# A DCN ranking kernel: row fetches for ScalarE, copies of transposed values for VectorE, another order on TensorE

## What is computed

```python
D = 26 * 64
x0 = emb[ids].reshape(ids.shape[0], -1)          # ids past the table take its last row
x = x0
for i in range(3):
    s = x @ cross_w[i]
    x = x0 * s[:, None] + cross_b[i] + x
h = relu(x0 @ w1 + b1)      # 1664 -> 1024
h = relu(h @ w2 + b2)       # 1024 -> 512
h = relu(h @ w3 + b3)       # 512 -> 256
y = sigmoid(concatenate([x, h], axis=1) @ out_w + out_b)
```

## Time and profile before

| | us |
|---|---|
| median of 3 runs | 549.64 (549.58 to 550.9) |
| the profiled execution | 547.23 |
| its span, first to last instruction | 545.4 |
| TensorE busy (matmul) | 478.0 (88%) |
| GpSimd busy | 391.6 (72%) |
| VectorE busy | 182.8 (34%) |
| ScalarE busy | 103.8 (19%) |

### The profile page before, as it was taken

How to read it: one execution, slowest core, us unless ns; L and a number is a source line. 1 busy time by engine, 2 the same in 40 slices (tenths; PEclk the granted TensorE clock), 3 DMA queues, 4 the chain that set the end, 5 groups by cost and what they waited for, 6 DMA issues and landing times.

```text
span 545.4 us, 10919 instructions
## 1 busy us (share of the span) xinstructions
PE 478.0 (88%) x2876; PEld 438.4 (80%) x2876; DVE 182.8 (34%) x380; ACT 103.8 (19%) x187; POOL 391.6 (72%) x412
## 2 busy tenths in 40 slices
PE   0079599999989989997999989999899989999997
PEld 0069499998978879896888979788798968888896
DVE  5464623232242323223332312323232233323324
ACT  6486511011011111101111101111111011111111
POOL 5777567777777777777777777777777777777730
PEclk9999899999999999999999989999999999999999
DMA  7992111111111111111111111111111111111100
GB/s 231 223 360 74 22 25 28 26 29 28 27 28 26 30 26 29 29 28 29 27 27 30 28 29 29 26 28 28 26 28 29 30 25 29 28 26 28 27 14 2
DMA packets 20608, 25.15 MB, mean 46 GB/s; under 512 B 10135, under 2 KB 11122, under 8 KB 20546
## 3 DMA queue, kind: packets, MB, share of 16 engines
q0 software_dynamic: 12960, 13.30, 13.6%
q1 hardware_dynamic: 6288, 10.94, 5.9%
q10 hardware_dynamic: 1298, 0.21, 0.2%
HBM read 24.41 MB, written 0.01 MB: 45 GB/s over the span
## 4 chain that ended last, share of the span: by engine, by line
PE 57%; POOL 14%; DMA 11%; DVE 9%; issue 8%; ACT 2%; POOLq 0%; DVEq 0%; ACTq 0%
PE l_bank L700 45%; POOL x_raw L334 14%; DMA x_raw<-in_L_rec_emb,idx 10%; PE h_bank L700 5%; PE x_bank L714 4%; DVE x_raw L510 4%; DVE h L529 3%; PE l_bank L774 1%; ACT w_hi L352 1%; PE h_bank L785 1%; ACT h_bank L362 1%; DVE w_lo L495 1%; DMA ids<-in_r_ids 0%; PE h_bank L740 0%; DVE h1T_lo L522 0%
## 5 line engine op out<-in xcount | busy, mean ns | idle before, releaser
L334 POOL DMA_INDIRECT x_raw<-in_L_rec_emb,idx x405 | 390.7, 965 | 131.1 <-issue 108.8
L700 PE MATMUL l_bank<-w_hi,xT_hi 128*128 128x342 f32 (+1 forms) x624 | 144.8, 333 | 8.2 <-DVE xT_lo L517 8.2
L700 PE MATMUL l_bank<-w_lo,xT_hi 128*128 128x342 f32 (+1 forms) x624 | 139.0, 323 | 0.0
L700 PE MATMUL l_bank<-w_hi,xT_lo 128*128 128x342 f32 (+1 forms) x624 | 138.7, 323 | 0.0
L700 PEld LDWEIGHTS l_bank<-w_hi,xT_hi 128*128 128x128 f32 x624 | 105.4, 193 | 10.9 <-issue 5.0
L700 PEld LDWEIGHTS l_bank<-w_lo,xT_hi 128*128 128x128 f32 x624 | 108.1, 193 | 0.0
L700 PEld LDWEIGHTS l_bank<-w_hi,xT_lo 128*128 128x128 f32 x624 | 107.2, 191 | 0.0
L510 DVE COPY_PREDICATED x_raw<-past,end_row 128x256 f32<-128x256 int32 (+3 forms) x65 | 40.5, 624 | 164.2 <-DMA x_raw<-in_L_rec_emb,idx 164.0
L398 ACT ACTIVATE xT_hi<-x_bank 128x512 fp32r<-128x512 f32 (+3 forms) x66 | 33.5, 507 | 270.5 <-PE x_bank L714 263.3
L714 PE MATMUL x_bank<-identity,x_raw 128*128 128x128 f32 x208 | 35.0, 280 | 46.3 <-DVE x_raw L510 28.8
L714 PEld LDWEIGHTS x_bank<-identity,x_raw 128*128 128x128 f32 x208 | 23.9, 142 | 58.2 <-issue 57.6
(11 more groups left out here) (83 smaller groups left out, 280.8 us busy)
## 6 DMA issues: line engine op xcount, KB each, us to landing
ids<-in_L_rec_emb SPq DMA_DIRECT2D x896, 0.2 KB
w_raw<-in_L_rec_w SPq DMA_DIRECT2D x18, 512.0 KB, 22.2
ids<-in_L_rec_emb ACTq DMA_DIRECT2D x512, 0.2 KB
x_raw<-in_L_rec_emb,idx POOLq DMA_INDIRECT x405, 2.5
b_rows<-in_L_rec_b SPq DMA_DIRECT2D x1, 512.0 KB, 7.5
b_rows<-in_L_rec_b SPq DMA_DIRECT2D x1, 256.0 KB, 5.7
ids<-in_r_ids SPq DMA_DIRECT2D x1, 208.0 KB, 2.6
b_rows<-in_L_rec_b SPq DMA_DIRECT2D x1, 128.0 KB, 6.7
```

Source lines behind the costliest of these rows:

```text
L334: pool.indirect_dma_start(out=dst, out_offset=None, in_=emb, in_offset=rows).then_inc(landed, 16)
L700: done = pe.matmul(bank[:, 0:b - a], x[:, k, :], w[:, k, a:b], start=(k == 0 and n == 0), stop=(k == last_k and n == 2))
```

## The change

- GpSimd gathers 399 fields instead of 405. SyncE fetches field 24 of nine tiles, with 32 registers a load and byte addresses. ScalarE fetches field 25 of eight tiles, 32 registers a load, one field after the other.
- From tile 1 on ScalarE does nothing but these fetches up to the last tile. Its copies of transposed values (x, h1, h2) and of the side buffers become VectorE copies, each right before the VectorE subtraction that needs it. In the last tile the copies of transposed values are ScalarE's again.
- The end row is copied into the last 64 columns of the PSUM bank `x_bank[1]`, and `make_whole` reads it there.
- Groups are of 4, 3, 4 and 2 chunks. In the last tile chunk 12 comes before chunks 9 to 11.
- TensorE's list: the first half of l2 of the tile before stands ahead of the transposition of group 0, which waits for `h3_ready`; a transposition of rows stands one or two chunks before the end of the group before; layer 3 comes at the end of the next tile and writes into `x_bank[0]`.
- GpSimd's wait for `l3_done` moves from field 6 to field 16.
- The end: layer 2's first half of columns is finished first, its transposition lies in the second half, the second half is transposed in two single chunks, and the last sum of the last tile is done by ScalarE with its sigmoid.

The diff, cut to its core:

```diff
-    SIZES = [4, 4, 3, 2]
+    SIZES = [4, 3, 4, 2]
...
-    LAST_SIZES = [4, 3, 2, 2, 1, 1]
-    LAST_GROUPS = [list(range(sum(LAST_SIZES[:g]), sum(LAST_SIZES[:g + 1]))) for g in range(len(LAST_SIZES))]
-    assert sum(LAST_SIZES) == K1
+
+    LAST_GROUPS = [[0, 1, 2, 3], [4, 5, 6], [7, 8], [12], [9, 10], [11]]
+    assert sorted(sum(LAST_GROUPS, [])) == list(range(K1))
...
-    SP_TILES = [3, 5, 7, 9, 11, 13, 15]
+    SP_TILES = [2, 4, 6, 8, 9, 10, 12, 14, 15]
+    SP_REGS = 32
...
-    ACT_TILES = [4, 7, 10, 13]
+    assert SP_FIELD // FPK in GROUPS[-1] and SP_FIELD // FPK in LAST_GROUPS[3]
+    ACT_RUNS = [[3, 5], [6, 8, 10], [11, 13], [14]]
+    ACT_TILES = sum(ACT_RUNS, [])
     ACT_FIELD = F - 1
     ACT_BUFS = 2
-    ACT_REGS = 16
-    ACT_SHARES = [12, 4, 8, 8, 12]
-    assert ACT_FIELD // FPK in GROUPS[-1] and all(
-        sum(ACT_SHARES) * (t - 1) >= P * (j + 1) for j, t in enumerate(ACT_TILES)) and ACT_TILES[-1] < TILES - 1
+    ACT_REGS = 32
+    assert ACT_FIELD // FPK in GROUPS[-1] and TILES - 1 not in ACT_TILES
...
+        end_bank = x_bank[1][:, 512 - E:512]
...
-        l3_bank = h_bank[1]
+        l3_bank = [x_bank[0]] * (TILES - 1) + [h_bank[1]]
...
-                for p in range(0, P, len(regs)):
-                    sync.load(regs, sp_idx[i:i + 1, p:p + len(regs)])
+                for p in range(0, P, SP_REGS):
+                    regs = [sync.alloc_register(f"sp_row{i}_{p + j}") for j in range(SP_REGS)]
+                    sync.load(regs, at_bytes[at_row[t]:at_row[t] + 1, p:p + SP_REGS])
                     for j, reg in enumerate(regs):
-                        row = sync.snap(reg, min_val=0, max_val=H - 1)
-                        sync.dma_start(sp_rows[i % SP_BUFS][p + j:p + j + 1, :],
-                                       emb[bass.DynSlice(row, 1), :]).then_inc(sp_landed[i % SP_BUFS], 16)
-            sync.wait_ge(result_ready, 1)
+                        at = sync.snap(reg, donate=True, min_val=0, max_val=(H - 1) * ROW)
+                        sync.dma_start(sp_rows[i % SP_BUFS][p + j:p + j + 1, :].bitcast(U8),
+                                       emb_bytes[:, bass.DynSlice(at, ROW)]).then_inc(sp_landed[i % SP_BUFS], 16)
...
-                if f == 6 and t > 2:
-                    pool.wait_ge(l3_done, t - 1)
                 if f == 14:
                     pool.wait_ge(l1_done, len(PIECES) * (t - 1) + 1)
                 if f == 16:
                     pool.wait_ge(h1_transposed, 2 * t)
+                    pool.wait_ge(l3_done, t - 1)
                     pool.wait_ge(x_transposed, NG * t + 1)
...
+            def fetch(j):
+
+                if j >= ACT_BUFS:
+                    act.wait_ge(act_placed, j - ACT_BUFS + 1)
+                row = len(SP_TILES) + j
+                for p in range(0, P, ACT_REGS):
+                    regs = [act.alloc_register(f"act_row{j}_{p + i}") for i in range(ACT_REGS)]
+                    act.load(regs, at_bytes[row:row + 1, p:p + ACT_REGS])
+                    for i, reg in enumerate(regs):
+                        at = act.snap(reg, donate=True, min_val=0, max_val=(H - 1) * ROW)
+                        act.dma_start(act_rows[j % ACT_BUFS][p + i:p + i + 1, :].bitcast(U8),
+                                      emb_bytes[:, bass.DynSlice(at, ROW)]).then_inc(act_landed[j % ACT_BUFS], 16)
...
-            act.wait_ge(sp_idx_ready, 2)
-            for t in range(1, TILES - 1):
-                step(t)
+            act.wait_ge(sp_idx_ready, 1)
+            for j in range(len(ACT_TILES)):
+                fetch(j)
             last_step(TILES - 1)
             act.wait_ge(logits_ready, 1)
-            act.activation(result[:, :], logits[:, :], ACT.Sigmoid).then_inc(result_ready, 1)
+            act.activation(result[:, 0:TILES - 1], logits[:, 0:TILES - 1], ACT.Sigmoid).then_inc(result_ready, 1)
+            act.wait_ge(h3_read, TILES)
+            act.activation(result[:, TILES - 1:TILES], h3_dots[:, TILES - 1:TILES], ACT.Sigmoid,
+                           bias=term[:, TILES - 1:TILES]).then_inc(result_ready, 1)
...
-                                    end_row[:, :].rearrange("p (o e) -> p o e", o=1).broadcast_to([P, n, E])).then_inc(x_whole, 1)
+                                    end_bank.rearrange("p (o e) -> p o e", o=1).broadcast_to([P, n, E])).then_inc(x_whole, 1)
+
+            def x_hi(t, g):
+                dve.wait_ge(x_transposed, NG * t + g + 1)
+                ks = groups(t)[g]
+                dve.tensor_copy(xT_hi[:, ks[0]:ks[-1] + 1, :].rearrange("p k b -> p (k b)"),
+                                x_bank[g % 2][:, 0:len(ks) * P]).then_inc(xT_hi_ready, 1)
+
+            def relu_hi(bank, cols, hi, done):
+                dve.tensor_scalar(hi, bank[:, 0:cols], 0.0, None, ALU.max).then_inc(done, 1)
+
+            def h1_hi(t):
+                for half in range(2):
+                    dve.wait_ge(h1_transposed, 2 * t + half + 1)
+                    relu_hi(h_bank[half], HB * P, h1T_hi[:, half * HB:(half + 1) * HB, :].rearrange("p k b -> p (k b)"), h1T_hi_ready)
+
+            def h2_hi(t):
+                dve.wait_ge(h2_transposed, t + 1)
+                relu_hi(h_bank[0], K3 * P, h2T_hi[:, :, :].rearrange("p k b -> p (k b)"), h2T_hi_ready)
+
+            def place(rows, t, field, placed):
+                dve.tensor_copy(x_buf[t % 2][:, field * E:(field + 1) * E], rows).then_inc(placed, 1)
+
+            def sp_place(t):
+                i = SP_TILES.index(t)
+                dve.wait_ge(sp_landed[i % SP_BUFS], 16 * P * (i // SP_BUFS + 1))
+                place(sp_rows[i % SP_BUFS], t, SP_FIELD, sp_placed)
+
+            def act_place(t):
+                j = ACT_TILES.index(t)
+                dve.wait_ge(act_landed[j % ACT_BUFS], 16 * P * (j // ACT_BUFS + 1))
+                place(act_rows[j % ACT_BUFS], t, ACT_FIELD, act_placed)
...
+            def step(t):
+                make_whole(t, 0)
+                x_hi(t, 0)
                 x_lo(t, 0)
+                l2_out(t - 1)
                 make_whole(t, 1)
-                l2_out(t - 1)
+                x_hi(t, 1)
                 x_lo(t, 1)
+                h2_hi(t - 1)
+                h2_lo(t - 1)
                 make_whole(t, 2)
-                h2_lo(t - 1)
+                x_hi(t, 2)
                 x_lo(t, 2)
-
-            def step(t):
-                begin(t)
+                if t in SP_TILES:
+                    sp_place(t)
+                if t in ACT_TILES:
+                    act_place(t)
                 make_whole(t, 3)
-                l3_out(t - 1)
+                x_hi(t, 3)
                 x_lo(t, 3)
                 l1_out(t)
                 dots_out(t)
-                make_whole(t + 1, 0)
+                h1_hi(t)
                 h1_lo(t)
+                l3_out(t - 1)
...
+                if g == 0 and t > 1:
+                    pe.wait_ge(h3_ready, t - 1)
...
+            def l2_last(t, half, ks):
+                for k in ks:
+                    if half == 0 and k % QB == 0:
+                        pe.wait_ge(h1T_ready, 2 * t + 1 + k // QB)
+                    for n, (x, w) in enumerate(((h1T_hi, w2_hi), (h1T_hi, w2_lo), (h1T_lo, w2_hi))):
+                        done = pe.matmul(L2_LAST[half][:, 0:NH], x[:, k, :], w[:, k, half * NH:(half + 1) * NH],
+                                         start=(k == 0 and n == 0), stop=(k == K2 - 1 and n == 2))
+                    if k == K2 - 1:
+                        done.then_inc(l2_done, 1)
...
+            def ahead(t):
+                return 1 if t >= TILES - 2 else 2
...
-
+                l2(t - 1, range(0, HB))
                 transpose_x(t, 0)
-                l2(t - 1, range(0, HB))
+                l2(t - 1, range(HB, K2))
                 l1(t, 0, slice(0, 1))
-                l2(t - 1, range(HB, K2))
+                transpose_h2(t - 1)
+                l1(t, 0, slice(1, -ahead(t)))
                 transpose_x(t, 1)
-                l1(t, 0, slice(1, 3))
-                transpose_h2(t - 1)
-                l1(t, 0, LAST)
-                l1(t, 1, slice(0, 1))
-                transpose_x(t, 2)
-                l3(t - 1)
-                l1(t, 1, slice(1, None))
+                l1(t, 0, slice(-ahead(t), None))
 
             def step(t):
                 begin(t)
+                for g in range(1, NG):
+                    l1(t, g, slice(0, -ahead(t)))
+                    if g < NG - 1:
+                        transpose_x(t, g + 1)
+                    l1(t, g, slice(-ahead(t), None))
+                transpose_h1(t)
+                l3(t - 1)
+
+            def last_step(t):
+                begin(t)
+                l3(t - 1)
+                l1(t, 1, BODY)
+
+                pe.wait_ge(h3_ready, t)
+                transpose_x(t, 2)
+                l1(t, 1, LAST)
                 transpose_x(t, 3)
                 l1(t, 2)
+                transpose_x(t, 4)
                 l1(t, 3)
-                transpose_h1(t)
-
-            def last_step(t):
```

(22 more changed lines are left out.)

186 lines of the change are left out of this document (75 added, 111 removed).

## The result

The changed kernel takes 574.07 us (571.45 to 579.51) against 550.27 us for the kernel before: the ratio is 1.044, 95% interval 1.037 to 1.052. I had forecast 542.5. It is slower, by 24 us, and 32 us above my forecast.

The account below looks back on a forecast made before the run. GpSimd's gathers were taken as the bound from tile 3 on. Gathers and TensorE's remaining work gave a 534.1 us span, the late field 4.1 more (538.2), and run and median corrections 542.5 us; range of 8 in 10: 536 to 552.

Parts of the forecast that it names:

- the sum: Gathers to tile 14, then TensorE's remaining work: span 534.1 us, 538.2 with the late field, 542.5 at the median.
- 3.4 us later: Tile 14: TensorE transposes group 2 at 479.8 us, 3.4 us after the gather of field 21 starts at 476.4.
- from tile 3 on its gates open 1 to 6 us early: GpSimd's waits on TensorE cost nothing from tile 3 on; it loses 2.1 us once, in tile 2.
- the late field: Tile 14's field fetched by ScalarE lands by 489.6 us, needed by 485.5: 4 us late, added to the end in full.
- ScalarE can't keep the pace: Rival, ScalarE's row fetches: over 0.422 us a row, tile 14's field makes the kernel slower than before; chance 0.13.
- End row in PSUM: VectorE's L510 reads one source from PSUM and no longer stretches 20 gathers: some 7.3 of 8.1 us come back.
- Placed copies: 17 fp32 SBUF copies moved to VectorE, 0.21 us each, could hold gathers: 3.6 us at most, likelier a few tenths.
- Copies to VectorE: Seven copies a tile at 0.68 us add 4.4 us to VectorE; TensorE waits 0.3 us, covered by the gathers' pace.
- the gates on free buffers never bind: ScalarE's fetches never wait for a free buffer: the fetch for tile 6 starts at 169 us, tile 3 is placed at 140.
- the stretches stay: Rival: L510 still stretches gathers, which come 7.3 us later and hide the late field: 545.7 us; chance 0.15.
- VectorE holds TensorE: Rival: VectorE's serial copies cost TensorE over 1.5 us of waiting a tile instead of 0.4 and become the bound; chance 0.07.
- Rows in time: Rival: a ScalarE load of 32 costs like one of 16 or little more, so gathers set the time: 538.4 us; chance 0.22.

Follow-up runs that it names:

- the two controls: The kernel before with the end row in PSUM and groups of 4, 3, 4, 2: 539.33 us; with those groups alone: 546.57 us.
- the comparisons above: Four ScalarE fields, 403 gathers each: the changed kernel, 542.55 us; the kernel before with end row in PSUM and SyncE's nine fields, 536.65 us.

## Why the prediction was wrong, point by point

**The bound.** Right for the kernel before, and for each variant in which the rows' rate is low: 401 to 407 gathers at 1.25 us set the time. In the kernel without ScalarE's rows the mean distance of gathers after the hundredth is 1.249 us (519.9 for the last start).

**The step that failed** is in the sum, at "3.4 us later": the time from the last gather of a group to TensorE's transposition, 3.26 us in the earlier trace rows, of which 2.45 are the landing. I took it over unchanged into a kernel with 49% more rows per us (4.9 instead of at most 3.3). Measured, the landing alone was 3.7 to 10.9 us. It holds TensorE, then GpSimd's gates hold the gathers, so a lag that a single group would pay once is paid in every tile. With it fell "from tile 3 on its gates open 1 to 6 us early": from the hundredth gather on GpSimd stopped 14 times, for 37.5 us together, and the last gather starts at 545.1. From the kernel without ScalarE's rows it would have been 519.9 - 8 x 1.25 = 509.9, 35 us earlier. In the terms of the sum: field 21 of tile 14, which I had at 476.4, starts at 511.4, 35.0 us late; from there to the end it took 58.2 us, where the sum without the late field has 57.7; and the 4.1 us of the late field were not paid. 538.2 + 35.0 + 0.5 - 4.1 is the measured span of 569.7 to 0.1 us. So one step, with the gates behind it, makes up the error.

I priced more rows only as a matter of the issuing queue, as c per row, with ScalarE's longest issue of 0.514 against 0.235 in view; whether that row had to do with a full engine no run shows. The issue did not slow down: 0.235 median again, and 52.2 to 54.6 us a field. The landings behind it did. No rival of mine had it; "ScalarE can't keep the pace" names the right resource with the wrong mechanism, and 552 as the upper end came from it.

**End row in PSUM.** Right. No gather of the changed kernel was over 1.15 us, where the earlier trace rows has one of 1.46. Of the size two readings stand: the two controls are 7.2 us apart, as the 7.3 that I had said; against the kernel before it is 5.3.

**Placed copies.** I had weighed them by the Trainium skill ("SBUF — State Buffer", section Who interferes with whom), by which a copy from SBUF to SBUF can block GpSimd, and whoever issues first blocks the other. The trace agrees in part. The copies held no gather, the gathers stay at 0.944; some copies waited. Those that started 0.60 to 0.70 us into a gather took 0.30 to 0.36 us, but those that started 0.07 to 0.42 us into one took 0.18, where I had said 0.21.

**Copies to VectorE.** Right in size (0.691 us for 512 columns; 0.68 was taken) and in effect: with the copies back on ScalarE nothing is won. TensorE's weight loads wait for h1T for 3.7 us in 15 pieces, 0.25 each, where 0.3 was worked out.

**GpSimd's stop at field 16 of tile 2.** Right: one stop, 2.6 us (I said 2.1). By the comparisons above the new order costs between this and some 6 us in all, for 0.4 us at the end: from the last h1 transposition to the end it is 13.0 us, after 13.4; I had counted on 0.9.

**ScalarE's pace.** Right to 1%: a load of 32 registers took 2.25 us (2.32 taken), a field 53.1 on average; SyncE's last row was issued at 504 (507 forecast). The Trainium skill ("Runtime: NRT & Kernel Launch", section Instruction fetch mechanics) has about 200 ns a register. The trace does not agree: the loads of 32, from SBUF, come to 70 ns each, so the case of far over 600 us doesn't happen. But "the gates on free buffers never bind" was wrong: ScalarE stood 17 us at 377, because tile 10 was placed late. And tile 14's field wasn't late: its last row was issued at 502.4, but by then the gathers were later than it. The 4 us that I had called the deciding term were never paid.

**The rivals.** That the stretches stay and that VectorE holds TensorE did not happen. "Rows in time" came out half by luck: the fetched rows did come in time, but because the gathers were late, and not because a load of 32 was cheap.

## What to carry to other kernels

When work is moved to a DMA queue, ask not only whether the issuing engine has the time but which DMA engines the transfers land on: here many DMAs of one partition all waited in one place, and gathers spread over sixteen parts waited for the one that was behind. Leave such a stream a margin (here 3.9 rows per us cost nothing, 4.5 a little, 4.9 cost 35 us and more), or let each DMA cover sixteen partitions. A landing time read from the trace belongs to the load under which it was read; a forecast that adds traffic must give it a range of its own.

## What the runs showed of the hardware that I had not expected

- Beside gathers of 128 rows each 1.25 us, single rows of 256 bytes at 4.9 per us make the last gather of a group land later by 2.6 to 3.0 us more every 100 us, up to 12.3 us in the chain; at 4.5 per us the landing stays at 4.8 or below. With 4 bytes a row at 4.9 it goes from 3.0 to 4.9 us in 260 us.
- It is one of a gather's sixteen parts that is late: fifteen increments within 2.3 us, the rest one by one, 1.4 us apart at the median.
- As many rows and bytes in DMAs of sixteen partitions cost nothing (544.64 us) where single ones cost 47 us.
- A row given as two or sixteen pieces takes its queue 0.54 to 0.64 us to issue instead of 0.23 (medians).
- With 128 bytes a row the same program ran at 548.69 us once and at 588 to 597 three times.
